# Counting edges in 18 tiles a block instead of 20, and turning the counts as bfloat16

## What is computed

```python
x = x + _L0_gnn_ref(_layernorm(x), batch0, edge_index, L0_gnn_W)
x = x + _L0_ffn_ref(_layernorm(x)[None], ...)[0]
x = x + _L1_gnn_ref(_layernorm(x), L1_gnn_W, ..., src, dst)
x = x + _L1_ffn_ref(_layernorm(x)[None], ...)[0]
```

```python
aw = jnp.einsum('ehf,ehf->eh', q[src], k[dest])     # one score for each edge and head
m = segment_max(aw, src); e = jnp.exp(aw - m[src])
out = segment_sum(e / segment_sum(e, src)[src] * v[dest], src)
```

## Time and profile before

| | us |
|---|---|
| median of 3 runs | 900.56 (898.99 to 901.5) |
| span of the profiled execution | 898.3 |
| the counting, first to last tile on TensorE | 44.7 to 163 |
| from there to the first step of the attention on VectorE | 163 to 186.6 |
| attention, first experts' start included | 186.6 to 510 |
| everything behind | 510 to 898.3 |

### The profile page before, as it was taken

How to read it: one execution, slowest core, us unless ns; L and a number is a source line. 1 busy time by engine, 2 the same in 40 slices (tenths; PEclk the granted TensorE clock), 3 DMA queues, 4 the chain that set the end, 5 groups by cost and what they waited for, 6 DMA issues and landing times.

```text
span 898.3 us, 16248 instructions
## 1 busy us (share of the span) xinstructions
PE 846.5 (94%) x5209; PEld 575.8 (64%) x5209; DVE 567.0 (63%) x1878; ACT 374.2 (42%) x680; POOL 206.3 (23%) x379
## 2 busy tenths in 40 slices
PE   6999998989999999999999899999988999996996
PEld 3456555447777777777777677777674445675664
DVE  6489999446777888788778365555534414875111
ACT  1234443446665566666556433334310012543331
POOL 4100000000021022012103241212236511465453
PEclk9999999999999999999999999999999999996998
DMA  9818988888101313111643827455135360175550
GB/s 261 319 28 200 209 215 204 130 303 212 34 26 30 106 54 95 42 53 25 230 128 106 262 67 214 155 178 160 60 92 128 82 197 12 35 244 129 166 172 24
DMA packets 87365, 121.02 MB, mean 135 GB/s; under 512 B 40782, under 2 KB 50158, under 8 KB 87022
## 3 DMA queue, kind: packets, MB, share of 16 engines
q1 hardware_dynamic: 73677, 101.82, 39.8%
q0 software_dynamic: 13600, 18.11, 7.3%
HBM read 65.52 MB, written 57.08 MB: 136 GB/s over the span
## 4 chain that ended last, share of the span: by engine, by line
PE 75%; DVE 12%; DMA 5%; issue 3%; ACT 2%; POOL 1%; SPq 1%; DVEq 0%; POOLq 0%; ACTq 0%
PE ps L787 17%; PE ps L678 10%; PE ps L707 10%; PE ps L917 9%; PE ps L689 8%; PE ps L568 5%; PE ps L944 4%; PE ps L794 4%; DVE R_B L1811 4%; DVE R_B L1810 2%; PE ps L573 2%; DMA R_A<-slots_d 1%; DVE R_A L1912 1%; PE ps L518 1%; DVE R_B L1806 1%
## 5 line engine op out<-in xcount | busy, mean ns | idle before, releaser
L787 PE MATMUL ps<-R_B,R_A 128*128 x612 | 184.6, 444 | 1.7 <-ACT R_A L1281 0.6
L787 PEld LDWEIGHTS ps<-R_B,R_A 128*128 128x128 f32 x612 | 111.2, 193 | 34.6 <-issue 24.5
L1217 ACT ACTIVATE R_A<-R_A,neg_max 125x1250 f32<-125x1250 f32 x80 | 106.6, 1333 | 58.2 <-DVE neg_max L1912 58.2
L1912 DVE CUSTOM_DVE_ANT_0 R_A<-ps,R_B,neg_max 125x417 f32<-125x417 f32 (+1 forms) x160 | 97.6, 648 | 29.1 <-PE ps L678 29.1
L678 PE MATMUL ps<-R_B 64*125 64x417 f32 (+1 forms) x480 | 106.5, 544 | 3.1 <-DVE neg_max L1912 1.6
L707 PEld LDWEIGHTS ps<-R_W,XN 125*64 125x64 f32 x1600 | 85.3, 136 | 23.1 <-issue 23.0
L689 PE MATMUL ps<-ident,R_A 125*125 125x125 f32 x800 | 98.7, 278 | 0.0
L689 PEld LDWEIGHTS ps<-ident,R_A 125*125 125x125 f32 x800 | 94.9, 188 | 1.5 <-DVE R_W L1919 0.7
L707 PE MATMUL ps<-R_W,XN 125*64 125x125 f32 x1600 | 94.7, 272 | 0.0
L1224 ACT ACTIVATE R_W<-ps 125x500 f32<-125x500 f32 x120 | 66.1, 585 | 51.3 <-PE ps L689 51.3
L1811 DVE TENSOR_SCALAR R_B<-R_B 125x418 bf16<-125x418 uint16 x200 | 77.2, 386 | 0.0
(11 more groups left out here) (269 smaller groups left out, 1178.0 us busy)
## 6 DMA issues: line engine op xcount, KB each, us to landing
slots_d<-R_B SPq DMA_DIRECT2D x9, 2322.0 KB, 12.4
R_B<-in_L_ffn_w_dram SPq DMA_DIRECT2D x28, 512.0 KB, 7.4
R_A<-slots_d SPq DMA_DIRECT2D x27, 256.0 KB, 2.8
slots_d<-R_A SPq DMA_DIRECT2D x27, 256.0 KB, 2.6
counts_d<-R_A SPq DMA_DIRECT2D x10, 546.9 KB
logs_d<-R_B SPq DMA_DIRECT2D x10, 546.9 KB
R_B<-logs_d SPq DMA_DIRECT2D x10, 546.9 KB
R_B<-counts_d SPq DMA_DIRECT2D x10, 546.9 KB
```

Source lines behind the costliest of these rows:

```text
L787: ins = pe.matmul(bank(b, TM, width), lhs[:, c * TM:c * TM + TM], flat[:, bass.ds(e * (n * width) + c * width, width)], start=c == 0, stop ...
L1217: act.activation(SC[u % 2][h], SC[u % 2][h], ACT.Exp, bias=neg_max[:, 2 * (u % 2) + h:2 * (u % 2) + h + 1], scale=-1.0, accum_out=den[:, 2 ...
L1912: dve.tensor_tensor_reduce(SC[u % 2][h][:, a:z], bank(2 * h + g % 2, P, z - a), LNB[i % 2][:, a:z], -1.0, least if t else 3.0e38, ALU.add, ...
```

## The change

A window has 18 tiles instead of 20, cut into parts of 6, 6 and 6 instead of 7, 7 and 6. On the fast path ScalarE writes the copied counts as bfloat16 (`CT_b`, over the same memory), TensorE turns them against a bfloat16 identity `ident_b` into bfloat16 in PSUM, and ScalarE's move to `stage`, which stays fp32, reads them from there. GpSimd makes `ident_b` once at the start. The general path keeps fp32.

```diff
-WIN = 20
+WIN = 18
-WINDOW_PARTS = ((0, 7), (7, 14), (14, 20))
+WINDOW_PARTS = ((0, 6), (6, 12), (12, 18))
...
+        CT_b = R_A[0:P, 1900:1900 + N // 2].bitcast(BF16)
+        ident_b = R_B[0:P, 17520:17584].bitcast(BF16)[:, 0:P]
...
+        def small_bank(b, n):
+
+            return bank(b, P, 64 * n).bitcast(BF16).rearrange("p (i n) -> p i n", i=n)
...
+            def turn_small_counts(b):
+
+                pe.wait_ge(S("ct_made"), b + 1)
+                above_zero(pe, S("ct_moved"), 3 * b)
+                for q, (a, z) in enumerate(TPIECES):
+                    for i in range(a, z):
+                        ins = pe.transpose(small_bank(2 + q, z - a)[:, i - a, 0:P], CT_b[:, i * P:i * P + P], ident_b)
+                    ins.then_inc(S("ct_turned"), 1)
...
-                            turn_counts(b - 1)
+                            turn_small_counts(b - 1)
...
-            def copy_counts(b):
+            def copy_counts(b, counts):
...
-                act.activation(CT, unpacked, ACT.Copy, accum_out=deg_in[:, bass.ds(b, 1)])\
+                act.activation(counts, unpacked, ACT.Copy, accum_out=deg_in[:, bass.ds(b, 1)])\
...
-            def counts_and_logs(b, k):
+            def turned_small_counts(q, n):
+
+                return small_bank(2 + q, n)[:, :, 0:P]
+
+            def counts_and_logs(b, k, turned):
...
-                    act.activation(stage[k][:, a:z, :],
-                                   bank(2 + q, P, (z - a) * P).rearrange("p (i n) -> p i n", n=P), ACT.Copy)\
-                       .then_inc(S("ct_moved"), 1)
+                    act.activation(stage[k][:, a:z, :], turned(q, z - a), ACT.Copy).then_inc(S("ct_moved"), 1)
...
+            pool.wait_ge(S("consts"), 1)
+            link(pool.tensor_copy(ident_b, ident[0:P, 0:P]))
```

More of the change, by code:

```diff
@@ L626, in _ @@
                         if b and part == 1:
-                            turn_counts(b - 1)
+                            turn_small_counts(b - 1)
                 project(28)
-                turn_counts(T - 1)
+                turn_small_counts(T - 1)
                 for n in range(29, 32):
@@ L1117, in move_packed, with turned_counts @@
                 act.activation(packed[:, 0:THIRD], bank(b % 2, P, THIRD), ACT.Copy).then_inc(S("packed_out"), 1)
-            def copy_counts(b):
+            def copy_counts(b, counts):
                 act.wait_ge(S("unpacked_out"), b + 1)
                 above_zero(act, S("ct_turned"), 3 * b)
-                act.activation(CT, unpacked, ACT.Copy, accum_out=deg_in[:, bass.ds(b, 1)])\
+                act.activation(counts, unpacked, ACT.Copy, accum_out=deg_in[:, bass.ds(b, 1)])\
                    .then_inc(S("ct_made"), 1)
-            def counts_and_logs(b, k):
+            def turned_counts(q, n):
+                return bank(2 + q, P, n * P).rearrange("p (i n) -> p i n", n=P)
+            def turned_small_counts(q, n):
+                return small_bank(2 + q, n)[:, :, 0:P]
+            def counts_and_logs(b, k, turned):
                 above_zero(act, counts_out[k], (b - k) * 16)
@@ L1186, in _ @@
                     if b:
-                        copy_counts(b - 1)
+                        copy_counts(b - 1, CT_b)
                     move_projected(pieces[1])
                     if b:
-                        counts_and_logs(b - 1, (b - 1) % 2)
+                        counts_and_logs(b - 1, (b - 1) % 2, turned_small_counts)
                     for n in pieces[2:]:
@@ L1193, in _ @@
                     move_packed(b)
-                copy_counts(T - 1)
+                copy_counts(T - 1, CT_b)
                 move_projected(28)
-                counts_and_logs(T - 1, (T - 1) % 2)
+                counts_and_logs(T - 1, (T - 1) % 2, turned_small_counts)
                 for n in range(29, 32):
@@ L1200, in _ @@
                 move_rest_ahead()
[L1201 to L1204, removed]
+                copy_counts(0, CT)
+                counts_and_logs(0, 0, turned_counts)
+                copy_counts(1, CT)
+                counts_and_logs(1, 1, turned_counts)
                 with act.Fori(1, T // 2) as h:
@@ L1207, in _ @@
                     for k in range(2):
-                        copy_counts(b + k)
-                        counts_and_logs(b + k, k)
+                        copy_counts(b + k, CT)
+                        counts_and_logs(b + k, k, turned_counts)
                 for n in range(6, 32):
```

## The result

The changed kernel takes 892.37 us (median of 6 runs, 890.13 to 893.41) against 900.77 us (6 runs, 898.99 to 904.03): ratio 0.99, 95% interval 0.988 to 0.9921. The forecast was 892.0. The gain of the medians is 8.4 us and the forecast sum 8.6, but the profiled spans differ by 7.2 only (898.3 and 891.1), and that is worth following: the traces hold a gain at the stores and a loss to the clock, neither of which was in the sum, and they partly cancel. The figures are of one traced execution of each kernel.

What follows compares the result with a forecast made beforehand. VectorE's one-hot pace bounds most windows, TensorE windows 5 and 6, then a serial chain up to the load. Two tiles (7.5 us) and faster turns (1.1) take 8.6 from 900.56: 892.0 us, range 889.9 to 894.6.

Steps and rivals of the forecast that it cites:

- the sum: Counting, window by window to the end of the tail: how much earlier each point comes, 8.6 us in all.
- The bound: Counting: VectorE paces most windows, TensorE windows 5 and 6, then a serial chain behind window 9 up to the load.
- The price of a turn: TensorE's turns in the counting: bfloat16 between 0.053 and 0.108 us, 0.06 taken, against 0.108 in fp32.
- The parts: Counting: two tiles less per window are worth 7.5 us, the bfloat16 type of the turns 1.1.
- The stores: Counting: a two-window round needs about 21.8 us, has 22.3, so fits; rival that they become the bound, 895.0 us, chance 0.09.
- Every later stage keeps its length.: Behind the counting: store wait, load, attention and all after keep their lengths; growth from 186.6 on would show the prediction wrong.
- a stretch at the low clock shifts: Behind the counting: a 1.2 GHz stretch falls on more or less work, 3.4 us either way, 888.6 or 895.4; chance 0.07.
- The slow rival: Counting: one block with 19 tiles would send all engines down the general path, above 1500 us; chance 0.01.

Runs made afterwards that it cites:

- e1: The kernel before with windows of 18 tiles, turns still in fp32; 894.8 us, ratio 0.9941 to the kernel before.
- e2: The changed kernel with windows of 20 tiles again, turns in bfloat16; 900.01 us, ratio 1.0001 to the kernel before.
- e5: The changed kernel with one projection moved from window 5 to window 3; 892.57 us, ratio 0.9924 to the kernel before.
- e7: The changed kernel with two projections each in windows 5 and 6, three in window 7; 893.27 us, ratio 0.9903 to the kernel before.
- e3: The changed kernel with 14 more idle products on TensorE ahead of the graph convolution; 892.67 us, ratio 0.992 to the kernel before.
- e8: e7 with block 9's counts moved before block 8's logarithm and unpacked before block 8 is masked; 891.59 us, ratio 0.9893 to the kernel before.
- e6: The changed kernel with one of the three late zeroings issued at block 7, before the last counts; 898.35 us in one execution.
- e4: The changed kernel with windows of 17 tiles, one less than block 6 touches; 1999.08 us in one execution.

## Why the prediction was right, point by point

- **The bound.** Right. VectorE paces windows 3, 4, 7, 8 and 9, TensorE windows 5 and 6, and the chain behind window 9 takes the rest. Openings against the sum: window 1 0.70 earlier (0.64), window 4 3.10 (3.04), window 5 4.03 (3.96), window 7 5.78 (5.72), window 9 7.63 (7.56), masking of block 9 8.73 (8.6). The error is 0.06 us from window 0 on, and that is the earlier beginning of the counting, not an error of the sum; 0.07 more come in the tail. So close an agreement of the counting is no luck: in the traces of e1, e2, e5 and e7 its length also changes by what was expected or by what the rival said, to 0.03 us.
- **The price of a turn.** Right: 0.057 us each, 0.06 taken. By the 81 ns that the Trainium skill gives ("TensorE: Matmul & The Clock Gate", Back-to-back issue gap), ten would take an estimated 0.81; they take 0.57. That the type would not matter was the prediction's inference from the page's section on transposes, which has no figure for fp32. The rate per column of other bfloat16 instructions in the same kernel gave the right value between the two bounds.
- **The parts.** Two tiles 7.5 and the type 1.1, measured 7.52 and 1.12 in the length of the counting. The times are less clear. On one chip the tiles alone give 894.8, a fall of 5.1 us, and kernels whose counting is as long as the changed one's 892.57 and 892.67 (e5, e3), falls of 7.3 and 7.2; the type alone gives none. Only the whole of the gain is shown by the times, its parts are shown by the traces.
- **The stores.** Right that they fit: the engines still stand idle for 2 us ahead of the counts of block 8, and the wait is not longer. The forecast put the threshold at 22.3 us a round. e7 has a round of 22.28 in windows 5 and 6 and its counting loses nothing; whether its longer store wait is a lack of room stays open. Where room does run short, in e8 and e6, it is at the end, among the last stores, which the sum by rounds didn't look at.
- **"Every later stage keeps its length."** This step failed, in size and not in the result, and one of the prediction's own signs of being wrong came true: the stretch from the attention on has grown, from 711.7 to 714.7 us. The store wait and the load came out 1.5 us shorter than in the earlier trace rows; e1 and e2 show 6.23 and 6.87 us for that wait, so the 8.08 was probably of that execution. And the rival "a stretch at the low clock shifts" happened beside the main case: 2.4 us lost at the start of the graph convolution, inside its plus or minus 3.4. 8.73 + 1.24 + 0.26 = 10.23 at the attention, less 2.4 at the graph convolution, less about 0.5 in the last mixture and 0.1 elsewhere, is the 7.2 of the spans. e1, e2, e5 and e7 take 713.5 to 715.0 us from the attention on without a low stretch at that place, so this length varies by the execution and no trace here ties it to the change.
- **The median.** It lies 0.4 us from the forecast. With single executions scattering over 890 to 893 us that is partly luck: the profile accounts for 7.2 us in one pair of executions, the medians for 8.4, and those of e3 and e5, in a series of their own, for 7.2 and 7.3. The prediction also took the 2.3 us between span and median for the launch; it is 1.7 (892.8 against 891.1 in the profiled execution), and the rest was the profiled execution's distance from the median. That left the forecast as it was, since the median was the base.
- **The slow rival** (19 tiles in a block) didn't occur; e4 shows its mechanism with a window one too small, and 1999 us is on the far side of the "above 1500".

**Left open.** Why the gap before the graph convolution is 3.33 us in one execution and 2.30 to 2.82 in the others; where the low stretches fall over many executions; whether e7's store wait is its own or the execution's; and whether the stores could be made faster. Rows of this case show them at 158 to 190 GB/s with full engines, nearly all packets under 512 bytes (2540 of 2544 from 162 to 169 after the change, 1.24 MB, so 488 bytes on average; the earlier trace rows, which the prediction names for its 500 bytes, have only the rate). The stretch of e7 from 177.6 to 184.4 moves 380 GB/s; that is the zeroing, also a store to DRAM, in packets of some 2 KB (1269 for 2.58 MB). The Trainium skill ("DMA: Bandwidth & Descriptors", Specifications) asks for at least 512 bytes for the full rate, and the two rates agree with that. But no run here stored the counts or logarithms in larger pieces, so the cause of their low rate is argued and not shown.

## What to carry to other kernels

Two engines busy 94% and 92% of a stretch say nothing about which one to relieve: find the window-by-window pace in the starts of one instruction that occurs once per window, and price each saving with the rate of the engine that rules that window. Time saved ahead of a store and a load arrives only if both still take as long and the engine behind them still has work until then: e7 shortened the counting by 2.32 us, 0.5 of it reached the attention, and TensorE, out of work for 2.22 us, lost 3.3 at the low clock. Look at the room of the stores and at the idle time of the next engine before a further saving. Traces can begin a stage at different times; subtract a common starting point before comparing hundredths. When two profiled spans differ from the sum by 2 or 3 us, compare stretch by stretch the granted clock and the long transfers first, and repeat the execution before you explain it.

## What the hardware showed that I had not expected

- A bfloat16 turn of 125 x 125 with weights of its own starts 57 ns after the last, and an fp32 one 108 ns, while single durations are 221 and 272 ns.
- ScalarE's three moves of the turned counts take as long from bfloat16 PSUM as from fp32. After and before:

```profile
105.96 1.34 ACT L1154 ACTIVATE R_A<-ps 125x500 f32<-125x500 bf16 x3 [0.77 <-PE ps L549]
```

```profile
110.84 1.34 ACT L1131 ACTIVATE R_A<-ps 125x500 f32<-125x500 f32 x3 [1.15 <-PE ps L534]
```

- Ahead of the graph convolution a lowered clock (0.50, 1.2 GHz) stands behind a gap of 3.33 us of TensorE and not behind seven gaps of 2.30 to 2.82; the 18 products then take 9.51 us instead of 7.81. At the attention's start it stands behind a gap of 2.22 already (e7). So the length of the last gap alone doesn't tell whether the clock falls.
